# Query norms as a stage of their own, query products spread over the batches, and the last key added after the output weights

## What is computed

```python
q = (hidden_states @ Wq).reshape(B, Sq, H, D)
k = (encoder_hidden_states @ Wk).reshape(B, Skv, H, D)
v = (encoder_hidden_states @ Wv).reshape(B, Skv, H, D)
q = rmsnorm(q, gq)
k = rmsnorm(k, gk)
scores = jnp.einsum('bqhd,bkhd->bhqk', q, k) * scale
attn = jax.nn.softmax(scores, axis=-1)
out = jnp.einsum('bhqk,bkhd->bqhd', attn, v)
return out.reshape(B, Sq, H * D) @ Wo
```

## Time and profile before

| | us |
|---|---|
| median of 3 runs | 2919.72 |
| lowest, highest | 2918.31, 2921.8 |
| profiled execution | 2916.03 |
| its span | 2914.2 |

### The profile page before, as it was taken

How to read it: one execution, slowest core, us unless ns; L and a number is a source line. 1 busy time by engine, 2 the same in 40 slices (tenths; PEclk the granted TensorE clock), 3 DMA queues, 4 the chain that set the end, 5 groups by cost and what they waited for, 6 DMA issues and landing times. The chain is left out here.

```text
span 2914.2 us, 51949 instructions
## 1 busy us (share of the span) xinstructions
PE 2624.2 (90%) x14275; PEld 2095.6 (72%) x14275; DVE 2102.3 (72%) x4976; ACT 1753.7 (60%) x3450; POOL 1110.5 (38%) x1357
## 2 busy tenths in 40 slices
PE   8999999999779999999999999999968778847998
PEld 6777777777657888888888888888853434335887
DVE  7999999999556667766666677766644666667886
ACT  6777777777545566655556666655652433315776
POOL 0100010011024444544444444544425565634775
PEclk9999999999889999999999999999987878767999
DMA  1000000100222222222222222222220001020111
GB/s 45 25 24 24 24 24 26 31 24 25 91 58 67 65 84 84 82 65 73 69 68 72 73 84 84 73 70 68 69 71 22 22 22 44 15 80 30 55 51 39
DMA packets 191005, 154.56 MB, mean 53 GB/s; under 512 B 20658, under 2 KB 186899, under 8 KB 190227
## 3 DMA queue, kind: packets, MB, share of 16 engines
q1 hardware_dynamic: 190866, 153.14, 18.5%
HBM read 138.38 MB, written 14.69 MB: 53 GB/s over the span
## 5 line engine op out<-in xcount | busy, mean ns | idle before, releaser
L251 DVE TENSOR_REDUCE kn_ssq<-kn_sq 128x8 f32<-128x1024 f32 x514 | 620.6, 1215 | 71.7 <-ACT kn_sq L193 65.3
L193 ACT ACTIVATE kn_sq<-kn_keys 128x1024 f32<-128x1024 f32 x514 | 527.9, 1027 | 177.1 <-PE kn_keys L142 174.6
L748 ACT ACTIVATE ca_sc<-ca_sc,ca_low 128x257 f32<-128x257 f32 x512 | 254.4, 499 | 251.5 <-DVE ca_low L868 251.5
L930 POOL TENSOR_TENSOR ca_sc<-ca_sc,ca_rden 128x1028 f32<-128x1028 f32 x128 | 243.3, 1901 | 407.1 <-DVE ca_rden L850 407.1
L142 PE MATMUL kn_keys<-kn_wk_hi,kn_ct_hi 128*128 128x512 f32 x1028 | 334.5, 406 | 1.0 <-ACT kn_sq L193 1.0
L142 PE MATMUL kn_keys<-kn_wk_lo,kn_ct_hi 128*128 128x512 f32 x1028 | 319.9, 392 | 0.0
L142 PE MATMUL kn_keys<-kn_wk_hi,kn_ct_lo 128*128 128x512 f32 x1028 | 319.7, 392 | 0.0
L676 PE MATMUL ca_b_out<-ca_vo,ca_oT 128*128 128x256 f32 x1024 | 245.9, 383 | 2.9 <-ACT ca_oT L756 0.7
L823 DVE CUSTOM_DVE_ANT_0 ca_sc<-ca_b_sc,ca_rk,ca_rq_rows 128x257 f32<-128x257 f32 x512 | 229.9, 482 | 5.4 <-PE ca_b_last L657 3.7
L142 PEld LDWEIGHTS kn_keys<-kn_wk_lo,kn_ct_hi 128*128 128x128 f32 x1028 | 193.3, 188 | 44.5
L142 PEld LDWEIGHTS kn_keys<-kn_wk_hi,kn_ct_lo 128*128 128x128 f32 x1028 | 193.2, 188 | 43.4
(11 more groups left out here) (281 smaller groups left out, 6640.4 us busy)
## 6 DMA issues: line engine op xcount, KB each, us to landing
ca_rk<-key_norms SPq DMA_DIRECT2D x512, 128.5 KB, 2.9
kn_rows<-in_ctx_dram SPq DMA_DIRECT2D x128, 128.0 KB, 2.4
ca_rows<-in_ctx_dram SPq DMA_DIRECT2D x128, 128.0 KB
ca_xin<-in_x_dram SPq DMA_DIRECT2D x32, 128.0 KB, 2.7
ca_xres<-in_x_dram SPq DMA_DIRECT2D x32, 128.0 KB, 3.1
x_after_attention<-ca_x SPq DMA_DIRECT2D x32, 128.0 KB, 2.8
tm_xg<-x_after_attention SPq DMA_DIRECT2D x8, 512.0 KB, 4.6
tm_xr<-x_after_attention SPq DMA_DIRECT2D x8, 512.0 KB, 4.9
```

Source lines behind the costliest of these rows:

```text
L193: act.activation(sq[c][:, :], keys[c][:, :], ACT.Square).then_inc(sq_ready, 1)
L251: dve.tensor_reduce(ssq[s][:, t * H + c * (H // 2):t * H + (c + 1) * (H // 2)], sq[c][:, :].rearrange("p (h d) -> p h d", d=P), AX.X, ALU. ...
L748: act.activation(sc[n][:, g, :], sc[n][:, g, :], ACT.Exp, bias=low[n][:, g:g + 1], scale=1.0, accum_out=den[n][:, g:g + 1]).then_inc(exp_r ...
L930: pool.tensor_tensor(sc[m][:, :, :], sc[m][:, :, :], rden[m][:, :].unsqueeze(2).broadcast_to((P, 4, SKV)), ALU.mult)\
```

## The change

- A new stage `query_norms` between the key norms and the cross attention walks over 32 tiles of 128 tokens. It normalises x, turns it, splits it, makes the queries (24 matmuls of 512 columns a tile), their squares and sums, and the roots (one power of 128 x 16 a tile, `inverse_root`). It stores the split columns and the norms to DRAM, and the attention loads both.
- Wq is split on GpSimd within `key_norms` (`split_queries`), no longer in the weight block.
- In the attention the `u` of the next superbatch is made ahead: pair n = bb - 1 in slot bb = 1 to 7, and pair 7 also in slot 7. The pairs go into `b_cols`, which the context columns use too; the new waits are `ulo_ready` in `turn_ctx` and `clo_ready` in `queries_ahead`. Before slot 0 of all there are 8 pairs in four banks.
- The 257th key takes no part in the values. Its weights of four batches are turned into four rows (`b_last[0:4]`), split, stored to DRAM and loaded as a block-diagonal stationary operand (`ps_diag`); the last context row times `vo` is made once for all batches (`vs_dram`), loaded for four batches, and added by two matmuls in output space. The column of the last key in the scores is copied by VectorE as before.
- `vo` and the values are split into high and low parts, and the output product becomes a triple (`out_lo` is the low part of the values).
- The loop over superbatches becomes one over pairs of them, 16 slots.

The diff, cut to what the prediction speaks of:

```diff
+            def split_queries(q):
+
+                for a in range(2):
+                    w = slice(q * CH // 2, (q + 1) * CH // 2)
+                    pool.wait_ge(wq_loaded, 16)
+                    pool.tensor_scalar(wq_hi[:, a, w], wq[:, a, w], 1.0, None, ALU.mult).then_inc(wq_split, 1)
+                    pool.wait_ge(wq_split, 4 * q + 2 * a + 1)
+                    pool.tensor_tensor(wq_lo[:, a, w], wq[:, a, w], wq_hi[:, a, w].bitcast(F32), ALU.subtract).then_inc(wq_split, 1)
+            for s in range(2):
+                inverse_root(s, s, 16 * s + 16)
+                split_queries(2 * s)
+                split_queries(2 * s + 1)
...
+def query_norms(nc, held, x_dram, wq_hi, wq_lo, xT_dram, rq_dram):
...
+            for t in range(TILES):
+                pe.wait_ge(xhi_ready, t + 1)
+                pe.wait_ge(xlo_ready, t + 1)
+                for c in range(PARTS):
+                    queries(t, c)
+                    if c == 0 and t + 1 < TILES:
+                        columns(t + 1)
...
+            x_hi(0)
+            normalise(1)
+            for t in range(TILES):
+                for c in range(PARTS):
+                    square(t, c)
+                    if c == 0 and t + 1 < TILES:
+                        x_hi(t + 1)
+                    if c == 1 and t + 2 < TILES:
+                        normalise(t + 2)
...
+                pool.wait_ge(qss_ready, PARTS * (t + 1))
+                ge(pool, rq_ready, 2 * t)
+                pool.tensor_scalar(ms[:, :], qss[t % 2][:, :], 1.0 / P, 1e-5, ALU.mult, ALU.add).then_inc(rq_ready, 1)
+                pool.wait_ge(rq_ready, 2 * t + 1)
+                pool.tensor_tensor(rq[:, t, :], ms[:, :], mhalf[:, :], ALU.pow).then_inc(rq_ready, 1)
+            inverse_std(0)
+            inverse_std(1)
+            for t in range(TILES):
+                if t + 2 < TILES:
+                    inverse_std(t + 2)
+                inverse_root(t)
...
+                if bb % 4 == 2 and live(quad(bb, r) - 1, QUADS):
+                    Q = quad(bb, r) - 1
+                    n = (bb // 4 + 1) % 2
+                    store_stray(Q, n)
...
+                if bb % 4 == 3 and live(quad(bb, r) - 1, QUADS):
+                    load_stray(quad(bb, r) - 1, (bb // 4 + 1) % 2, 32 * (2 * r + (bb // 4 - 1) // 2 + 1))
...
-            def queries(i):
...
-                        mm = triple(b_sc[n % 2][:, :], (xT_hi[:, a, s], xT_lo[:, a, s]), (wq_hi[:, a, r], wq_lo[:, a, r]), a == 0, a == 1)
...
-                            mm = triple(b_u[n % 4][:, k * TOK:(k + 1) * TOK], (qk_hi[:, a, h, :], qk_lo[:, a, h, :]),
-                                        (xT_hi[:, a, :], xT_lo[:, a, :]), a == 0, a == 1)
...
+                        mm = triple(bank[:, k * TOK:(k + 1) * TOK], (qk_hi[:, a, h, :], qk_lo[:, a, h, :]),
+                                    (x_columns(x, 0, a, odd), x_columns(x, 1, a, odd)), a == 0, a == 1)
...
+
+            def queries_ahead(b, bb, r, n):
+                odd = 1 - bb // PER
+                if n == 0:
+                    pe.wait_ge(xT_loaded[odd], 16 * (r + bb // PER + 1))
+                pe.wait_ge(clo_ready, b + 2)
+                if n == PER - 1:
+                    pe.wait_ge(ulo_ready, b + PER)
+                queries(b_cols, n, xT[odd], odd)
...
             def turn_ctx(b, bb):
...
                 ge(pe, clo_ready, b)
-                if bb % PER == 1:
-                    pe.wait_ge(xlo_ready, b // PER + 1 if isinstance(b, int) else turn_ctx.i + 1)
+                ge(pe, ulo_ready, pairs_before(b - 1, bb - 1) if not isinstance(b, int) or b > 0 else 0)
                 for a in range(2):
                     mm = pe.transpose(b_cols[:, a * P:(a + 1) * P], rows[n][:, a, :], ident[:, :])
...
+                c = bb % 4
+                if c == 0:
+                    ge(pe, pslo_ready, b // 4 if isinstance(b, int) else quad(bb, turn_p.r))
+                pe.transpose(b_last[0:4, c * P:(c + 1) * P], s[:, :, 2 * P], ident[:, :]).then_inc(p_turned, 1)
...
-                    triple(b_val[:, :], (row_hi[n][:, k, :], row_lo[n][:, k, :]), (pT_hi[:, k, :], pT_lo[:, k, :]), k == 0, False)
-                pe.matmul(b_val[:, :], last3[n][:, :], pl3[:, :], start=False, stop=True).then_inc(val_ready, 1)
...
+                    mm = triple(b_val[:, :], (row_hi[n][:, k, :], row_lo[n][:, k, :]), (pT_hi[:, k, :], pT_lo[:, k, :]), k == 0, k == 1)
+                mm.then_inc(val_ready, 1)
...
                 for h in range(4 * part, 4 * part + 4):
-                    mm = pe.matmul(b_out[:, 0:DIM], oT[n][:, h, :], vo[:, h, :], start=(h == 0), stop=(h == H - 1))
+                    triple(b_out[:, 0:DIM], (oT_hi[n][:, h, :], oT_lo[n][:, h, :]), (vo_hi[:, h, :], vo_lo[:, h, :]), h == 0, False)
                 if part == 3:
-                    mm.then_inc(out_ready, 1)
...
+                    pe.wait_ge(ps_loaded[n], 16 * 11 * uses)
+                    pe.matmul(b_out[:, 0:DIM], ps_diag[n][:, :], vs_rows[n][:, 0, :], start=False, stop=False)
+                    pe.matmul(b_out[:, 0:DIM], ps_diag[n][0:64, :], vs_rows[n][0:64, 1, :], start=False, stop=True).then_inc(out_ready, 1)
...
+                ahead = pairs_ahead(b, bb)
+                if ahead:
+                    queries_ahead(b, bb, r, ahead[0])
                 if live(b - 2):
                     values(b - 2, bb - 2)
...
+                if ahead[1:]:
+                    queries_ahead(b, bb, r, ahead[1])
...
+            for n in range(H // 2):
...
+                queries(b_u0[n % 4], n, xT[0], 0)
+            for k in range(H // 2):
+                ge(pe, vslo_ready, k - 1)
+                for v in range(2):
+                    mm = triple(b_p[k % 2][:, v * DIM:(v + 1) * DIM], (stray_hi[:, :], stray_lo[:, :]), (vo_hi[:, 2 * k + v, :], vo_lo[:, 2 * k + v, :]))
+                mm.then_inc(vs_ready, 1)
...
+                if live(b - 2) and (bb - 2) % 4 == 3:
+                    Q, n = quad(bb - 2, r), (bb - 2) // 4 % 2
+                    act.wait_ge(p_turned, 3 * (b - 2) + 3)
+                    ge(act, ps_stored[n], 32 * (2 * r + (bb - 2) // 8))
+                    act.activation(ps_hi[n][:, :], b_last[0:4, :], ACT.Copy).then_inc(pshi_ready, 1)
...
                     for g in range(4):
                         act.activation(sc[n][:, g, :], sc[n][:, g, :], ACT.Exp, bias=low[n][:, g:g + 1], scale=1.0,
                                        accum_out=den[n][:, g:g + 1]).then_inc(exp_ready, 1)
+                ahead = pairs_ahead(b, bb)
+                if ahead:
+                    act.wait_ge(sc_ready, 4 * b + 4)
+                    queries(b_cols, 1 - bb // PER, ahead[0], b + PER)
...
                     act.wait_ge(val_ready, b - 1)
...
+                        ge(act, out_ready, quad(bb - 2, r) - 1)
+                    act.activation(oT_hi[q][:, :, c * SQ:(c + 1) * SQ], b_val[:, :].rearrange("p (h q) -> p h q", q=SQ), ACT.Copy)\
+                        .then_inc(ohi_ready, 1)
+                if ahead[1:]:
+                    queries(b_cols, 1 - bb // PER, ahead[1], b + PER + 1)
...
+            def queries(bank, odd, n, done):
+                dve.wait_ge(uhi_ready, done)
+                dve.tensor_tensor(u_pair(u_lo, odd, n), bank[:, :].rearrange("p (h b q) -> p h b q", h=2, b=PER), u_pair(u_hi, odd, n).bitcast(F32),
+                                  ALU.subtract).then_inc(ulo_ready, 1)
...
+            def out_lo(b, bb, r):
+                c, q = bb % 4, bb // 4 % 2
+                dve.wait_ge(ohi_ready, b + 1)
+                if c == 0:
+                    ge(dve, out_ready, quad(bb, r) - 1)
+                w = slice(c * SQ, (c + 1) * SQ)
+                dve.tensor_tensor(oT_lo[q][:, :, w], b_val[:, :].rearrange("p (h q) -> p h q", q=SQ), oT_hi[q][:, :, w].bitcast(F32), ALU.subtract)\
+                    .then_inc(olo_ready, 1)
+
+            def slot(b, bb, r):
+                if live(b - 3):
+                    out_lo(b - 3, bb - 3, r)
...
-                    for k in range(3):
...
+                    for k in range(2):
...
                     dve.wait_ge(sc_used, 4 * b + 4)
                     dve.tensor_scalar(low[bb % 2][:, :], top[bb % 2][:, :], -1.0, None, ALU.mult).then_inc(low_ready, 1)
-                    split_last(b, bb)
...
+                if live(b - 2) and (bb - 2) % 4 == 3:
+                    Q, n = quad(bb - 2, r), (bb - 2) // 4 % 2
+                    dve.wait_ge(pshi_ready, Q + 1)
+                    dve.tensor_tensor(ps_lo[n][:, :], b_last[0:4, :], ps_hi[n][:, :].bitcast(F32), ALU.subtract).then_inc(pslo_ready, 1)
+                for k, n in enumerate(pairs_ahead(b, bb)):
+                    queries(b_cols, 1 - bb // PER, n, b + PER + k)
...
-    key_norms(nc, held, ctx, wk, rk)
-    cross_attention(nc, held, x, ctx, wq, wk, wv, wo, gq, gk, rk, x1)
+    with ExitStack() as st:
+        wq_raw = st.enter_context(nc.sbuf_tensor("wq_raw", [P, 2, wq.shape[1]], F32))
```

(4 more changed lines are left out.)

625 lines of the change are left out of this document (336 added, 289 removed).

## The result

The changed kernel takes 3028.39 us (median of 4 runs, 3026.78 to 3028.92) against 2919.01 us before (median of 4, 2916.5 to 2921.8): 1.037 times as long, 95% interval 1.036 to 1.039. The forecast was 3025 us. The profiled execution took 3028.66 us (span 3026.9), where the sum gave 3022.

A forecast was written before the change was run, and what follows sets the result against it. The prediction took the attention slot to be bound nearly equally by PE's work and a circle through in-order VectorE. Terms -137 + 244 - 7 + 6 = +106 us on 2916.0 gave 3022, forecast 3025 us, range 2950 to 3100.

The forecast's parts named there:

- query-norm stage: New stage before the attention: 32 tiles paced by waits through GpSimd, 226 us, plus ends and a border; term +244 us.
- weight stage: Block ahead of the attention: the splits of Wq move into the key norms, so it ends earlier; term -7 us.
- start of the attention: Before the first slot: eight pairs and eight last-key products with stores; first score 42.5 us in instead of 36.9; term +6.
- first to last scaled score: Cross attention from slot 0 to slot 127: 1149 us instead of 1285.5, superbatches of 73.1 us; term -137 us.
- The slot with a pair: Attention slots 1 to 6: a chain of waits through ScalarE, VectorE and PE sets a period of 8.95 us.
- The other slots: Attention: slot 7 with a second pair 11.95 us; slot 0 and the last superbatch's seven slots without pairs 7.47 us each.
- The circle through GpSimd: Query-norm stage: root, deviation, normalised tile, squares and sums wait on each other; 7.05 us a tile, power 2.94 us.
- The clock: PE's granted clock in the attention: left at 0.99 despite short idle gaps in the new slots.
- The rule of the Trainium skill: Attention: a PE idling briefly between groups of matmuls can swing between two clocks, so slots would lose time on top.
- Rival 1: Attention: PE stays the bound and waits are covered; about 57 us a superbatch, total 2741 us; chance 0.06.
- Rival 2: Attention: turned weights and scores are ready when VectorE asks; slots of 8.15 us, total 2930 us; chance 0.10.
- Rival 3: Attention: the clock drops between PE's groups in the slots; +135 us, total up to 3160 us; chance 0.08.

## Why the prediction was right, and where it was off

| term | predicted | measured |
|---|---|---|
| query-norm stage | +244 | 1019.47 - 774.54 = +244.9 |
| weight stage | -7 | 34.1 - 40.9 = -6.8 |
| start of the attention | +6 | 35.3 - 36.6 = -1.3 |
| first to last scaled score | -137 | 1164.2 - 1289.2 = -125.0 |
| rest | 0 | 773.8 - 772.9 = +0.9 |
| sum | +106 | +112.7 |

The borders are the first transfer of the weight stage, the first of the attention, and the first and last scaled score (those of before: 852.1 and 2141.3). SP's queue in the timeline of the kernel before:

```profile
774.54 0.38 SPq L355 DMA_DIRECT2D ca_wq<-in_L_xattn_Wq_dram  x1
...
815.46 0.33 SPq L559 DMA_DIRECT2D ca_stray<-in_ctx_dram  x1
```

and of the changed one:

```profile
1019.47 0.38 SPq L551 DMA_DIRECT2D ca_wq<-in_L_xattn_Wq_dram  x1
...
1053.56 0.33 SPq L801 DMA_DIRECT2D ca_stray<-in_ctx_dram  x1
```

The scaled scores of the changed kernel (durations in ns, first and last start):

```profile
L1020 DVE CUSTOM_DVE_ANT_0 ca_sc<-ca_b_sc,ca_rk,ca_rq_rows x512: 476/482/490, 1088.9 to 2253.1; 128x257 f32<-128x257 f32 x171
```

and of the one with its loop written out:

```profile
L1018 DVE CUSTOM_DVE_ANT_0 ca_sc<-ca_b_sc,ca_rk,ca_rq_rows x512: 475/481/486, 1086.9 to 2228.4; 128x257 f32<-128x257 f32 x171
```

**The slot with a pair: right, step for step.** Predicted 8.95 us, found 8.96 (8.86 in the superbatches outside the loop). The high part starts at 2.19 (2.19 predicted), the low part is done at 3.49 (3.51), PE turns at 3.55 (3.57), the first scaled score comes at 5.54 (5.41), and from there it takes 3.42 (3.54): errors of 0.13 and 0.12 that cancel, so that the slot came out to 0.01 us is partly luck. That this is the cause and not only the picture is shown by three edits at three links of the circle: own bank (-86 us), earlier pair (-107), later context (-115).

**The other slots: sizes off.** Slot 0 took 6.93, not 7.47; the last seven 7.2 to 7.5; slot 7 took 12.04 where it is written out, 11.95 predicted. Not counted were, in slot 5 (9.15 us outside the loop against 8.86), the two output products of the last key, behind which the third group of scores stands in PE's order: VectorE waits 0.2 us for it there, and without the last key the slot is as short as the others. In slot 1 (9.12) the negated maximum takes 0.43 us instead of 0.17; why is open. The residual add (L1042, 0.41 us ahead of the reciprocal in slots 2 and 6) costs nothing in slots with a pair, since it lies under PE's way, and 0.3 us in each of two of the last seven (7.5 against 7.2). Much more was the loop: 0.1 us a slot, 0.6 in slot 7 and 1.1 to 2.4 at each of five edges. Without the loop the stretch from first to last score is 2228.4 - 1086.9 = 1141.5 us, 22.7 less than with it. The kernel before also spends some 10 us on its loop. The term of -137 was mis-sized by 12 us: its own working without the loop is 10 us too long (1149 us from the first score of slot 0 to that of slot 127, measured 1139), and the loop, which it put at nothing, adds 23.

**The start: mis-sized by 7.** The stores of the last key's values were taken as 3.5 us to land and 5.3 a round, from a load of twice the size. They land in 2.1, and a round of four stores takes 3.5; there are four rounds. The first store of three rounds in the timeline:

```profile
1072.70 0.36 SPq L811 DMA_DIRECT2D last_values<-ca_pT_hi  x1
...
1076.27 0.33 SPq L811 DMA_DIRECT2D last_values<-ca_pT_hi  x1
...
1079.77 0.33 SPq L811 DMA_DIRECT2D last_values<-ca_pT_hi  x1
```

and the row of these transfers (count, KB each, us to landing):

```profile
last_values<-ca_pT_hi SPq DMA_DIRECT2D x8, 256.0 KB, 2.1
```

**The query-norm stage: right in cause, and in size by two errors that cancel.** The circle through GpSimd was worked out as 7.05 us a tile; it is 6.81 to 6.93; the power took 2.917 us, 2.94 predicted from a line through two others. The tiles took 32 x 6.81 = 218 us instead of 226, the ends 27 instead of 18: 8 too much and 9 too little, so that +244 met +244.9 is luck. One number in one line takes the circle away and 34 us with it; PE's 188 us of work are the most of what remains, and they were only moved here. In the same way the sum of all terms (3022 for 3028.7) is so near because the start's 7 us too many and the attention's 12 too few partly cancel.

**The clock: left at 0.99, found at 0.99.** PE idles (1162 - 937) / 128 = 1.8 us a slot here, and the granted clock was 0.99 over the 1162 us; in the slots between the edges of the loop it did not fall. The rule of the Trainium skill that was weighed against this ("TensorE: Matmul & The Clock Gate", "A second HAM failure mode") did not take hold in these slots. Behind the edge of the loop shown above, where PE had idled 2.84 us, its eight turned weights took 1.92 us (1676.96) instead of 1.04 (1627.11), and the granted clock of these five microseconds was 0.66, so the lower of its two levels (1.2 GHz) came up there:

```profile
1675.00:1680.00 5.00, 3.51 (x20) 3.43 (x21) 0.89 (x5) 1.47 (x3) 1.73 (x1) 0.66 0.40 114
```

So it went at the next two edges (idle 2.52 and 2.37 us, 1.91 us for the turned weights, 0.66). At the first (2.56 us) the clock was 0.88 over 1375 to 1380 and the turned weights were not slower, and at the second (2.74 us) it was 1.00. The three edges with slow turned weights took 14.7 to 15.0 us, the other two 13.7 and 13.9: the clock is about 0.9 us of the dear ones.

**The rivals.** Rival 1 (PE bound, 2741 us) is near what the layout could give: with the orders put right it is 2799, with the loop written out and the plain product 2761. Rival 2 did not occur by itself; taking PE's share out of the circle gave 2938 (own bank) and 2914 (later context), where 2930 was worked out for it, with slots of 7.78 us instead of the 8.15 worked out. Rival 3 occurred at the edges alone and at the very start.

## What to carry to other kernels

- An engine executes in order, so a wait belongs behind everything that doesn't need it. The change put a product's consumer (the low part of the pair) ahead of PE's turned weights and scores, which need nothing of it; moving two transposes behind them gave back 115 us without another bank or another operation.
- When work is spread into the gaps of a loop, follow one circle of waits through all engines with the durations that the old trace shows. Here that told the slot to 0.01 us (its two halves to 0.13), and it named the links that an experiment could cut one by one.
- A slow operation (here a power of 2.9 us on GpSimd) can cost only through its place in another engine's order. Look two steps down the chain for the instruction that stands behind it.
- Compare slots as well as times. Here a loop cost 14 to 37 us depending on what stood in it, which hid a gain of 16 us in one experiment.

## What the hardware showed that was not expected

- **The edge of a loop stops all engines.** In a body of 16 slots each jump back cost 1.1 to 2.4 us in the changed kernel, and 3.3 to 4.2 in the one without the last key; with all waits against registers gone too, the three kernels gained 29, 28 and 10 us. The Trainium skill ("Advanced Engine Details and Errata", "ISA Cache") speaks of cache lines of 16 KB or 256 instructions and of only two of them; that the jump goes back to instructions that are no longer held there would fit. The instruction transfers in the trace speak for it: the queue q8 brings packets of 16 KB, and at each of the five edges two of them come within 3.8 to 4.1 us, while with the loop written out no two in the attention are closer than 16.6. Over the whole kernel it moved more with the loop (first row: packets, MB, share) than without it (second):

```profile
q8 instruction: 96, 1.57, 0.2%
...
q8 instruction: 86, 1.41, 0.2%
```

In the kernel before, with 8 slots in the body, this queue brings nothing from 979 to 2073 us, so nothing is fetched again by it in that loop. That the engines wait for these packets is not shown; no run changed the length of the body alone.
